# A transformer layer with cross-attention: k's stacks written through DRAM in 8 transfers, one run of 64 products with V per group

## The reference

```python
q, k, v = (x @ Wq + bq), (ctx @ Wk + bk), (ctx @ Wv + bv)      # split into 16 heads of 16
scores = einsum('bhqd,bhkd->bhqk', q, k) / sqrt(16)
scores = where(j < i, scores, -1e30)                            # strictly causal
attn = softmax(scores); attn[:, :, 0, :] = 0
y = layer_norm(x + (attn @ v) @ Wo + bo, ln1_g, ln1_b)
out = layer_norm(y + relu(y @ W1 + b1) @ W2 + b2, ln2_g, ln2_b) # W1 is 256 x 1024
```

## Time and profile before

| | |
|---|---|
| median of 3 runs | 1820.44 us |
| profiled execution | 1823.35 us |
| its span, first to last instruction | 1821.6 us |
| mean granted TensorE clock | 0.985 of full speed |
| PE busy / weight loads | 1740.5 us (96%) / 1635.5 us (90%) |
| DVE busy | 1451.6 us (80%) |
| ACT busy | 1454.9 us (80%) |
| POOL busy | 1346.5 us (74%) |
| DMA packets of SP's queue, share of 16 engines | 35.9% |

### The profile page before, as it was taken

How to read it: one execution, slowest core, us unless ns; L and a number is a source line. 1 busy time by engine, 2 the same in 40 slices (tenths; PEclk the granted TensorE clock), 3 DMA queues, 4 the chain that set the end, 5 groups by cost and what they waited for, 6 DMA issues and landing times.

```text
span 1821.6 us, 55434 instructions
## 1 busy us (share of the span) xinstructions
PE 1740.5 (96%) x17184; PEld 1635.5 (90%) x17184; DVE 1451.6 (80%) x6808; ACT 1454.9 (80%) x5697; POOL 1346.5 (74%) x1230
## 2 busy tenths in 40 slices
PE   3799999999999999999999999999999999999997
PEld 3699999999999999999999999999999899998997
DVE  4668878888887888877878878878887888887885
ACT  1778888888888888888888888888888888887883
POOL 2367777777777777777777777777777777777777
PEclk7889999999999999999999999999999999999999
DMA  6333343343333343344333333334343334333320
GB/s 159 87 97 101 85 108 104 83 108 103 83 108 104 84 108 106 80 107 105 81 106 107 80 108 104 83 107 107 81 107 106 80 108 107 80 107 106 79 67 24
DMA packets 186244, 175.68 MB, mean 96 GB/s; under 512 B 43360, under 2 KB 161120, under 8 KB 185952
## 3 DMA queue, kind: packets, MB, share of 16 engines
q1 hardware_dynamic: 185952, 172.14, 35.9%
HBM read 54.53 MB, written 16.78 MB: 39 GB/s over the span
## 4 chain that ended last, share of the span: by engine, by line
PE 92%; SPq 4%; issue 2%; DVE 1%; POOL 1%; DMA 0%; POOLq 0%; ACT 0%; DVEq 0%
PE ps_dense L342 29%; PE ps_dense L332 29%; PE ps_probsT L447 13%; PE ps_att L462 8%; PE ps_scores L437 7%; PE ps_dense L315 6%; SPq L246 2%; SPq L230 1%; DVE probs L635 0%; POOL hT L889 0%; DMA probs<-in_L_xattn_Wq_dram 0%; DVE u L768 0%; SPq L265 0%; DMA k_stack<-kT 0%; DVE u L801 0%
## 5 line engine op out<-in xcount | busy, mean ns | idle before, releaser
L520 ACT ACTIVATE probs<-ps_scores,negmax 128x128 f32<-128x128 f32 x2048 | 725.5, 379 | 74.3 <-DVE negmax L668 74.0
L881 POOL TENSOR_TENSOR probs<-probs,recip 128x512 f32<-128x512 f32 x512 | 533.4, 1047 | 286.3 <-DVE recip L662 286.2
L668 DVE CUSTOM_DVE_ANT_0 ps_scores<-ps_scores,mask 128x128 f32<-128x128 f32 x2048 | 531.1, 320 | 144.4 <-PE ps_scores L437 144.3
L520 ACT ACTIVATION_READ_ACCUMULATOR probs<-ps_scores,negmax 128x1 f32 x2048 | 451.0, 220 | 0.0
L332 PE MATMUL ps_dense<-zT,w 128*128 128x256 f32 x3072 | 413.5, 284 | 0.5 <-DVE h_f L738 0.5
L342 PE MATMUL ps_dense<-w,hT 128*128 128x256 f32 x3072 | 410.9, 283 | 0.4 <-POOL hT L889 0.4
L889 POOL TENSOR_TENSOR hT<-h_f,hT 128x512 fp32r<-128x512 f32 x256 | 330.0, 1289 | 91.2 <-DVE h_f L738 83.2
L332 PEld LDWEIGHTS ps_dense<-zT,w 128*128 128x128 f32 x3072 | 384.4, 189 | 0.9 <-issue 0.9
L342 PEld LDWEIGHTS ps_dense<-w,hT 128*128 128x128 f32 x3072 | 381.0, 188 | 0.6 <-issue 0.6
L447 PE MATMUL ps_probsT<-ident,probs 128*128 128x128 f32 x2048 | 316.4, 277 | 0.1
L532 ACT ACTIVATE probsT<-ps_probsT 128x508 f32<-128x508 f32 x512 | 312.3, 610 | 2.9 <-PE ps_probsT L447 2.9
(11 more groups left out here) (74 smaller groups left out, 2287.8 us busy)
## 6 DMA issues: line engine op xcount, KB each, us to landing
q_stack<-qT SPq DMA_DIRECT2D x768, 64.0 KB, 2.4
k_stack<-kT SPq DMA_DIRECT2D x1536, 32.0 KB, 2.0
x_tok<-in_x_dram SPq DMA_DIRECT2D x64, 256.0 KB, 3.0
c_tok<-in_ctx_dram SPq DMA_DIRECT2D x64, 256.0 KB, 3.1
x_res<-in_x_dram SPq DMA_DIRECT2D x64, 256.0 KB, 4.7
out_dram<-o_tok SPq DMA_DIRECT2D x64, 256.0 KB, 2.3
probsT<-in_L_xattn_W_dram SPq DMA_DIRECT2D x1, 1024.0 KB, 8.5
u<-in_L_xattn_W_dram SPq DMA_DIRECT2D x2, 256.0 KB, 2.9
```

The source lines that it names most:

```text
L520: last = nc.scalar.activation(probs[:, m % 4, i, :], ps_scores[m % 2][:, i, :], ACT.Exp, bias=negmax[:, m % 4, i:i + 1], scale=-1.0, accum ...
L668: last = nc.vector.tensor_tensor_reduce(ps_scores[m % 2][:, i, :], ps_scores[m % 2][:, i, :], mask[:], -1.0, -MASKED, ALU.add, ALU.min, ac ...
L881: nc.gpsimd.tensor_tensor(probs[:, m % 4], probs[:, m % 4], recip[:, m % 4, :].unsqueeze(2).broadcast_to([P, 4, S]), ALU.mult)\
```

## The change

Three things change together.

1. **k through DRAM.** `spill_k` writes the high half of `kT` (128 partitions of 2 KB, so 256 KB, in one transfer) to a DRAM scratch tensor `k_spill`, and the low half likewise: 2 transfers. `stack_k` reads them back into the layout of the stacks with 6 transfers of 16 partitions by 8 rows of 1 KB. The second waits for the first to land (`k_hi_in_dram`, `k_lo_in_dram`). 8 transfers take the place of 24. Both `scores(g, 0)` and `scores(g, 1)` now wait for all of k's.
2. **One run of products with V.** `probsT` has 12 unit buffers. `attend(g)` is called once per group, after unit 7 of the group has been copied, and fills the whole bank `ps_att`; `att_hi` and `att_lo` move all 512 columns at once instead of 256 twice.
3. **New orders** on all five engines, and new `BANK` and `HELD_BY`.

```diff
+NPT = 12
-BANK = {"xT": 0, "zT": 1, "v": 1, "q": 1, "cT": 0, "f1_0": 1, "k": 0, "f1_1": 2, ...
+BANK = {"xT": 1, "zT": 0, "v": 2, "q": 1, "cT": 0, "f1_0": 0, "k": 0, "f1_1": 1, ...
...
+        k_dram = nc.dram_tensor("k_spill", (2, 2, KC, P, GT), F32).ap()
+        k_rows = k_dram.rearrange("n h c (j e d) t -> n h e d (c j) t", j=4, e=2)
...
-        probsT = sb("probsT", [P, 4, 4, S])
+        probsT = sb("probsT", [P, NPT, 4, S])
...
-            def stack_k(g, i, part):
+            def spill_k(g, part):
                 if exists(g):
                     if part == 0:
                         sp.wait_ge(s_hi["k"], KC * (g + 1))
                     else:
                         sp.wait_ge(taken["k"], KC * (g + 1))
+                    need(sp, s_kstack, 16 * 2 * PARTS * (g - 1))
+                    sp.dma_start(k_dram[g % 2, part].rearrange("c p t -> p c t"), f32(kT[:, part])).then_inc(s_kspill[part], 16)
+
+            def stack_k(g, part):
+                if exists(g):
+                    sp.wait_ge(s_kspill[part], 16 * (g + 1))
                     need(sp, s_scores, (g - 1) * UNITS)
...
-                            for j in (2 * i, 2 * i + 1):
-                                for e in range(2):
-                                    sp.dma_start(
-                                        f32(k_stack[g % 2][32 * s + DK * e:32 * s + DK * (e + 1), j, :, e, :]),
-                                        f32(kT[32 * j + DK * e:32 * j + DK * (e + 1), half])).then_inc(s_kstack[i], 16)
+                            for e in range(2):
+                                sp.dma_start(f32(k_stack[g % 2][32 * s + DK * e:32 * s + DK * (e + 1), :, e, :]),
+                                             k_rows[g % 2, part, e]).then_inc(s_kstack, 16)
...
                 if m < 2:
                     pe.wait_ge(s_qstack[m], 16 * 2 * PARTS * (g + 1))
-                    pe.wait_ge(s_kstack[m], 16 * 4 * PARTS * (g + 1))
+                    pe.wait_ge(s_kstack, 16 * 2 * PARTS * (g + 1))
...
-            def attend(g, m):
+            def attend(g):
...
+                pe.wait_ge(s_pTsb, (g + 1) * UNITS)
+                pe.wait_ge(taken["v"], g + 1)
+                need(pe, s_att_lo, g)
+                for b in range(GB):
+                    for c in range(KC):
+                        for e in range(2):
+                            for j in range(4):
+                                unit = (g * UNITS + 4 * b + 2 * c + j // 2) % NPT
...
-                need(act, s_att, g * (UNITS // 2) + m // 2 - 1)
-                nc.scalar.activation(probsT[:, m % 4, :, 1:S], ps_probsT[m % 2][:, :, 1:S], ACT.Copy).then_inc(s_pTsb, 1)
+                need(act, s_att, (g * UNITS + m - NPT) // UNITS + 1)
+                nc.scalar.activation(probsT[:, (g * UNITS + m) % NPT, :, 1:S], ps_probsT[m % 2][:, :, 1:S], ACT.Copy).then_inc(s_pTsb, 1)
...
-                c_hi(it + 2)
-                att_hi(it, 0)
+                exponentials(it + 1, 0)
+                q_hi(it + 2)
...
             def iteration(it):
-                q_lo(it + 1)
+                c_lo(it + 1)
                 norm1(it - 2)
...
```

More of the change, by code:

```diff
@@ L102, in encoder_layer @@
         q_stack = [sb(f"q_stack{i}", [PARTS * 32, 4, KC, GT], F32R) for i in range(2)]
-        k_stack = [sb(f"k_stack{i}", [PARTS * 32, 4, KC, 2, GT], F32R) for i in range(2)]
+        k_stack = [sb(f"k_stack{i}", [PARTS * 32, 4 * KC, 2, GT], F32R) for i in range(2)]
         v_sb = [sb(f"v_sb{i}", [P, GB, PAIRS, 3, DK]) for i in range(2)]
         probs = sb("probs", [P, 4, 4, S])
-        probsT = sb("probsT", [P, 4, 4, S])
+        probsT = sb("probsT", [P, NPT, 4, S])
         negmax = sb("negmax", [P, 4, 4])
@@ L155, in encoder_layer @@
         s_qstack = [sem(f"q_stacked{i}") for i in range(2)]
-        s_kstack = [sem(f"k_stacked{i}") for i in range(2)]
+        s_kspill = [sem(f"k_{half}_in_dram") for half in ("hi", "lo")]
+        s_kstack = sem("k_stacked")
         s_scores = sem("scores_ready")
@@ L267, in iteration @@
             def iteration(it):
[L268 to L272, removed]
-                next_x(it + 3)
[L274 to L277, removed]
+                next_c(it + 3)
+                next_x(it + 3)
+                spill_k(it + 2, 1)
+                stack_k(it + 2, 0)
+                stack_k(it + 2, 1)
+                stack_q(it + 2, 1)
+                load_residual(it + 1)
+                store(it - 2)
+                stack_q(it + 3, 0)
+                spill_k(it + 3, 0)
             load_weight(0)
@@ L448, in probs_transpose @@
                 last.then_inc(s_pT, 1)
-            def attend(g, m):
+            def attend(g):
                 if not exists(g):
                     return
[L453 to L466, removed]
+                pe.wait_ge(s_pTsb, (g + 1) * UNITS)
[6 more added lines that the diff above has]
+                                unit = (g * UNITS + 4 * b + 2 * c + j // 2) % NPT
+                                last = nc.tensor.matmul(
+                                    ps_att[32 * j:32 * j + 32, (c * GB + b) * S:(c * GB + b + 1) * S],
+                                    v_sb[g % 2][:, b, 4 * c + j, e:e + 2, :],
+                                    probsT[:, unit, 2 * (j % 2) + e, :],
+                                    start=(e == 0), stop=(e == 1), tile_position=(0, 32 * j), skip_group_check=True)
                 last.then_inc(s_att, 1)
@@ L568, in k_hi @@
                 if exists(g):
-                    for i in range(2):
-                        need(act, s_kstack[i], 16 * 4 * PARTS * g)
+                    for part in range(2):
+                        need(act, s_kspill[part], 16 * g)
                     projection_hi(g, "k", kT, bk_col)
```

142 lines of the change are left out of this document (68 added, 74 removed).

## The result

The changed kernel takes 1768.38 us, the median of 4 runs (1766.0 to 1769.79), against 1820.69 us before (4 runs). The ratio is 0.9713, 95% interval 0.9696 to 0.973: 52 us, 2.9% faster. I had forecast 1693, with 1672 to 1755 as the range. The direction was right and the size was not: less than half of the forecast gain arrived, and 1768 lies outside the range.

What follows compares the result with a forecast made beforehand. SP's full queue was taken to set the 27.28 us period, PE 0.7 behind. 1821.6 - 109 (steady part) - 16 (head) - 1 (group 2) - 5 (tail) = 1691 for the span; forecast 1693 us, range 1672 to 1755.

Steps and rivals of the forecast that it cites:

- SP as the pace of the kernel before: SP's full queue of 40 transfers sets the 27.28 us period; PE is 0.7 us per group behind it.
- The run of V products: On PE, one run of 64 takes 1.9 us instead of 3.0 for four calls: 1.1 us per group saved.
- PE's own sum: PE's work per group without waits: 26.6 - 3.0 + 1.9 = 25.5 us, taken as the new period.
- Place (b): DVE from scores 7 through maxima, c_lo and norm1: done at 25.25, PE's transpose of z wants it at 25.8; margin 0.5 us.
- rival B: A wait on ACT or DVE takes the old waits' place, 0.5 to 0.8 us per iteration: 1724, up to 1742; chance 0.13.
- Place (a): ACT's fourth h_hi ahead of unit 5's exponentials, which unit 7's scores need: done at 21.1 against 22.0, margin 0.9 us.
- Place (c): k's trip through DRAM, 6.7 to 9.4 us from k_lo to last landing, ahead of unit 0's scores: margin 2 to 4.7.
- Head and tail: Before and after the steady part: head 16 us less, group 2 another 1 less, tail 4 to 5 less.
- The prediction's own test: The period between scores of unit 0 is 25.5 us; the forecast is wrong if it is above 26.

Runs made afterwards that it cites:

- the cut in four: The POOL edit with the run of 64 V products cut into four parts of 16, other PE work between and wo behind the last W1 quarter: 1813.27 us, ratio 0.99.
- the POOL edit: Changed kernel with POOL waiting until both norm1 instructions on DVE are done, and scale_z2 moved behind normalise: 1723.88 us, ratio 0.9465.

## Why the prediction was wrong

**SP as the pace of the kernel before: right.** Taking the k transfers off its queue alone gave 55 us on that chip: 0.7 per period and 10 in the head (scores of group 2 at 78.7 instead of 89.6).

**The run of V products: right.** It takes 1.89 us from start to start, as forecast. What it saves was 0.15 us too good: 0.94 us per group by the cut in four, not 1.1, since the one run still costs its neighbours 0.2. The Trainium skill's rule that a change of tiling mode drains the array (TensorEngine Tiling (Array Packing), Key Properties) agrees: three entries more cost 0.9 us with the same 64 records.

**PE's own sum: 25.5 forecast, 25.86 measured** with every wait gone. I gave all twelve dense blocks 1.42. Five take 1.50 to 1.53: the three that stand between a transpose of the probabilities and a score pair (900.97 to 902.48 is one), the one behind the transpose of z (903.81 to 905.32) and the one behind the V run. They add 0.44; the other terms together come out 0.08 lower. Worth 61 x 0.36 = 22 us.

**Place (b), the step that failed.** I gave norm1 "two of 0.59, started 0.52 apart, 1.1" and found a margin of 0.5 us. Measured: 2.39 us, so 1.3 more than given, which turns the margin of 0.5 into -0.8; and at that transpose PE stands idle 0.5 us, its weight loads 0.7, in every group. The other terms of the place came out: from the start of scores 7 to that of norm1 there are 2.08 us (925.45 to 927.53), where I had 2.15. Worth 61 x 0.69 = 42 us, 44 by the POOL edit. The 0.59 was a mean over two kinds of instances, 0.40 and about 1.1 us, of one instruction whose duration depends on what POOL does at that moment; and the new POOL order puts three instructions back to back exactly there (scale_z2, normalise, offset_z2). The trace of the kernel before already showed it: of the four in a row, the first two stood beside POOL's normalise and took 0.40 and 1.13 us, the last two beside an idle POOL and took 0.40 each. I had rival B for "a wait on ACT or DVE takes the place", with 0.13 and 1724 to 1742, but it allowed for rows 0.5 to 1 us late, not for a pair of instructions over twice as long as given.

The Trainium skill has the rule (SBUF — State Buffer, SBUF: two separate sides): DVE and GpSimd share one pair of SBUF ports under an exclusive lock, held for the whole instruction, when the DVE instruction runs in a two-port mode, or has two SBUF inputs beside a GpSimd instruction that reads SBUF. The trace agrees: beside POOL 1.25 to 1.34 us for TENSOR_SCALAR from SBUF to SBUF and 1.40 to 1.48 for two sources, against 0.53 with one side in PSUM; the mode that an instruction ran in stands in no row. I hadn't weighed it in the prediction. An estimate with the durations of POOL's two instructions in that place, 1.0 and 1.3 us, would have made the pair 2.3 instead of 1.1 and the margin at (b) negative.

**Place (a)** held: no wait of the scores for ACT is left in the steady part. **Place (c)** held, with less room than forecast: the trip took 9.8 us (median; up to 11.2) instead of at most 9.4, because k_stack lands in 4.6 us and the spill in 3.4; the margin was 1.6 (at least 0.4), not 2 to 4.7. Making it longer wasn't tried, so the point at which it decides stays computed.

**Head and tail:** group 2 at 79.0 instead of 73 (the first scores at 32.7, forecast near 30), tail 69.2 instead of 67.9 - 5 = 62.9, together 12 us. No run looks for the reason. The sum of the errors: 61 x (26.55 - 25.5) = 64, 12, and 1 of rounding, are the 77 us between the forecast span of 1691 and the 1768.0 measured. Of the 64, 42 are place (b) and 22 PE's own sum. The prediction's own test, "wrong if the period is above 26", caught it.

## What to carry to other kernels

Before a duration goes into a sum, look at its minimum, median and maximum: here a TENSOR_SCALAR from SBUF to SBUF, or a TENSOR_TENSOR with two sources in SBUF, has one duration on DVE while POOL is idle and another while it is busy, until POOL's instruction ends. When an order is changed, check who runs beside whom at the narrow places, not only who waits for whom. And when two limits lie close together (27.28 and 26.6 us here), a gain on the second is worth something only if every chain ahead of it was walked with the slow durations; idle time given to POOL at the right place was worth 44 us and a swap of two lines on DVE 34, beside the 52 of the whole change.

## What the runs showed of the hardware that I had not expected

- Two DVE instructions on 2 columns took 0.99 and 1.33 us where the same two on 256 columns took 1.10 and 1.36, when POOL was in a row of instructions. DMA traffic made no difference (404 against 406 ns).
- Which of the two begins first matters. In the changed kernel norm2's first instruction begins at 914.28, 0.16 us ahead of a POOL instruction, and takes 0.39 us; that POOL instruction takes 1.12 instead of 1.04.
- BATCH_NORM_STATS2 kept its 0.41 to 0.43 us beside POOL, though both its ends are in SBUF.
- Loads issued beside k's transfers lengthened the spill (3.4 against 2.5 us) but not the 16-partition reads into k_stack (4.6 both times).
